# RWKV attention and fp4 feed-forward layer: the scores of all heads in one run, the down projection at the end of the step

## The reference

```
xx = [x(second row), x shifted by one row] - x
r, k, v = (x + xx*mix_{r,k,v}) @ W_{r,k,v}.T ;  g = sigmoid((x + xx*mix_g) @ W_g.T)
for each of 16 heads of width 16, over t:   state = state*w + k_t v_t^T ;  out_t = state r_t
y  = (out * g) @ W_o.T
x1 = layernorm(x + layernorm(y)*gamma + beta)
q(z) = blockwise fp4 quantise/dequantise, blocks of 16
h  = silu(q(x1) @ q(w_gate).T) * (q(x1) @ q(w_up).T)          (704 wide)
out = layernorm(x1 + q(h) @ q(w_down).T)
```

## Time and profile before

| | |
|---|---|
| median of 3 runs | 659.39 us (658.94 to 662.06) |
| profiled execution, its own time | 656.57 us |
| its span in the trace | 654.6 us |
| PE busy | 569.1 us (87%) |
| DVE busy | 510.9 us (78%) |
| POOL busy | 330.4 us (50%) |
| ACT busy | 277.2 us (42%) |
| mean granted clock | 0.959 of 2.4 GHz |

### The profile page before, as it was taken

One profiled execution on the slowest core, in us unless ns is written; L12 is line 12 of the kernel. 1 busy time (PEld: TensorE's weight loads), 2 busy tenths in 40 slices (PEclk: granted clock), 3 DMA queues, 4 the chain that ended last, 5 costly groups with the idle time before them and its releaser, 6 DMA issues.

```text
span 654.6 us, 14594 instructions
## 1 busy us (share of the span) xinstructions
PE 569.1 (87%) x5120; PEld 477.9 (73%) x5120; DVE 510.9 (78%) x1506; ACT 277.2 (42%) x637; POOL 330.4 (50%) x471
## 2 busy tenths in 40 slices
PE   1468589999999999999999999999999999987754
PEld 1356467888878888888888888888888888876643
DVE  2988667888878888888888888888788888778751
ACT  1235255444444455444445444444445544432211
POOL 2234344555555555555555555555565555544321
PEclk9687689999999999999999999999999999999896
DMA  7300000000000000000000000000000000000000
GB/s 191 102 2 1 9 10 3 1 18 17 19 17 18 18 17 19 18 17 18 17 11 9 17 18 19 18 17 17 18 18 18 9 11 10 9 10 10 9 9 20
DMA packets 14046, 13.13 MB, mean 20 GB/s; under 512 B 2576, under 2 KB 13712, under 8 KB 13968
## 3 DMA queue, kind: packets, MB, share of 16 engines
q1 hardware_dynamic: 13968, 12.13, 6.2%
HBM read 7.93 MB, written 4.19 MB: 19 GB/s over the span
## 4 chain that ended last, share of the span: by engine, by line
PE 79%; DVE 9%; ACT 5%; POOL 2%; issue 2%; DMA 1%; SPq 0%; DVEq 0%; POOLq 0%; ACTq 0%
PE bank L734 20%; PE bank L867 14%; PE bank L677 9%; PE bank L752 9%; PE bank L716 4%; PE bank L804 4%; PE bank L759 4%; PE bank L769 4%; PE bank L859 3%; ACT hq_t L591 3%; PE bank L704 2%; DVE mix L1044 2%; PE bank L694 1%; POOL rstd L353 1%; PE bank L814 1%
## 5 line engine op out<-in xcount | busy, mean ns | idle before, releaser
L371 POOL TENSOR_SCALAR_AFFINE_SELECT scores<-scores 128x512 f32<-128x512 f32 x128 | 89.0, 708 | 81.0 <-ACT scores L508 80.4
L867 PE MATMUL bank<-down_t,hq_t 128*128 128x256 f32 x384 | 94.1, 396 | 21.6 <-ACT hq_t L591 21.6
L353 POOL TENSOR_TENSOR rstd<-veps,neg_half 128x1 f32<-128x1 f32 x96 | 77.8, 810 | 66.9 <-DVE veps L994 66.1
L867 PEld LDWEIGHTS bank<-down_t,hq_t 128*128 128x128 f32 x384 | 72.0, 194 | 38.3 <-ACT hq_t L591 29.4
L1044 DVE SCALAR_TENSOR_TENSOR mix<-shift,mu,x_t 128x128 f32<-128x128 f32 x256 | 82.5, 374 | 2.6 <-POOL shift L380 2.6
L508 ACT COPY scores<-bank 128x512 f32<-128x512 f32 x128 | 68.8, 590 | 34.5 <-PE bank L677 32.7
L752 PE MATMUL bank<-mix,proj_t 128*128 128x128 f32 x512 | 70.2, 295 | 10.5 <-DVE mix L1044 10.5
L734 PE MATMUL bank<-gu_hi,xq_hi 128*128 128x352 f32 x256 | 68.4, 349 | 11.2 <-DVE late L1092 6.4
L380 POOL TENSOR_TENSOR shift<-x_t 128x256 f32<-128x256 f32 x32 | 20.1, 629 | 112.6 <-ACT x_t L529 111.3
L752 PEld LDWEIGHTS bank<-mix,proj_t 128*128 128x128 f32 x512 | 66.1, 209 | 12.1 <-DVE mix L1044 11.1
L677 PE MATMUL bank<-r_par,rv 32*128 32x256 f32 x512 | 72.5, 400 | 0.8 <-ACT scores L508 0.8
(11 more groups left out here) (123 smaller groups left out, 1160.2 us busy)
## 6 DMA issues: line engine op xcount, KB each, us to landing
x_tok<-in_L_attn_x_dram SPq DMA_DIRECT2D x32, 128.0 KB, 2.3
out_dram<-late_down SPq DMA_DIRECT2D x32, 128.0 KB, 1.7
late_down<-in_L_ffn_w_down_dram SPq DMA_DIRECT2D x1, 704.0 KB, 8.6
late<-in_L_ffn_w_gate_dram SPq DMA_DIRECT2D x1, 640.0 KB, 7.1
late<-in_L_ffn_w_up_dram SPq DMA_DIRECT2D x1, 640.0 KB, 7.3
scores<-in_L_attn_W_r_dram SPq DMA_DIRECT2D x1, 256.0 KB, 5.0
scores<-in_L_attn_W_v_dram SPq DMA_DIRECT2D x1, 256.0 KB, 5.3
scores<-in_L_attn_W_g_dram SPq DMA_DIRECT2D x1, 256.0 KB, 5.5
```

The lines of the kernel that those rows point to most:

```text
L353: g.tensor_tensor(rstd[:, i:i + 1], veps[:, i:i + 1], neg_half, ALU.pow).then_inc((rstd_ready, x_rstd, y_rstd)[i], 1)
L371: g.affine_select(out=a, in_=a, compare_op=ALU.is_ge, fill=0.0, base=0, pattern=[[0, 4], [1, P]], channel_multiplier=-1).then_inc(s_masked, 1)
L867: mm = t_.matmul(B_PA[:, 0:C], hq_t[:, t.c % 2, j], down_t[:, j], start=(j == 0), stop=(j == NH - 1))
```

## The change

- TensorE: the attention output (`outs_of`) now comes directly behind the state sums, and then the scores of all four quads in one run, into `B_PA`, `B_PB`, `B_S0` and `B_S1` (`s_bank`). Since `B_PA` and `B_PB` still hold r, v, g and k of `tile(1)`, the run waits for their readers: `rv_ready`, `r_par_ready`, `sg_ready`, `kd_ready`.
- TensorE: behind the first gate/up half come the transposes of hq (`tile(6)`), then that of v (`tile(1)`), then the second gate/up half, and the down projection last.
- ScalarE: the output norm ahead of the score copies; three score copies ahead of the first silu, the fourth behind it; then x1, the moves of hq_t, of v, and the second silu.
- GpSimd: the four masks together behind hq, the power of index 1 and gate_pow.
- VectorE: `norm1(1)`, `hgrid(3)`, `norm1(2)` and `u1` ahead of `norm3(2)`; `mix_of(R)` behind `norm2(1)`; `norm2(2)` ahead of `kd`; `mix_of(V)` behind `kd`.

```diff
--- before.py
+++ after.py
@@ -112,6 +112,7 @@
         bank = [ctx.enter_context(nc.psum_tensor(f"bank{i}", [P, 512], F32))[:] for i in range(8)]
         B_T, B_PA, B_PB, B_S0, B_S1, B_O, B_GATE, B_UP = bank
         w_bank = (B_GATE, B_UP)
+        s_bank = (B_PA, B_PB, B_S0, B_S1)
 
 
         ident = sb("ident", [P, P])
...
@@ -415,6 +410,8 @@
                                     ).then_inc(gate_pow_ready, 1)
                 t = None if general else tile(2)
                 if t is not None:
+                    mask(t, 0)
+                    mask(t, 1)
                     mask(t, 2)
                     mask(t, 3)
                 t = tile(4)
...
@@ -552,19 +549,23 @@
                     wait(act, tanh_ready, t.count(1, 1))
                     s.activation(sig_g[:, t.c % 2], sig_g[:, t.c % 2], ACT.Copy, bias=0.5, scale=0.5
                                  ).then_inc(sg_ready, 1)
+                t = tile(7)
+                if t is not None:
+                    wait(act, rstd2_ready, t.count(1, 1))
+
+                    wait(act, y_stored[t.c % 2], t.affine(16 * TPB // 2, 16 * (t.c // 2) + 1))
+                    normalised(y_out[:, t.c % 2], u2, 2, y_ready)
                 t = None if general else tile(2)
                 if t is not None:
                     score(t, 0)
                     score(t, 1)
-                t = tile(7)
-                if t is not None:
-                    wait(act, rstd2_ready, t.count(1, 1))
-
-                    wait(act, y_stored[t.c % 2], t.affine(16 * TPB // 2, 16 * (t.c // 2) + 1))
-                    normalised(y_out[:, t.c % 2], u2, 2, y_ready)
+                    score(t, 2)
                 t = tile(5)
                 if t is not None:
                     gate(t, 0)
+                t = None if general else tile(2)
+                if t is not None:
+                    score(t, 3)
                 t = tile(4)
                 if t is not None:
                     wait(act, x_norm_ready, t.count(1, 1))
...
@@ -592,6 +581,14 @@
                            ).then_inc(h_t_ready, 1)
                     s.copy(hq_t[:, t.c % 2, 4:6], B_PB[:, 0:256].rearrange("p (h n) -> p h n", h=2)
                            ).then_inc(h_t_ready, 1)
+                t = tile(1)
+                if t is not None:
+                    wait(act, v_tr, t.count(1, 1))
+                    wait(act, u_used, t.count(1, -3))
+                    s.copy(v_tok[:, t.c % 4], B_T[:, 0:C]).then_inc(v_tok_ready, 1)
+                t = tile(5)
+                if t is not None:
+                    gate(t, 1)
 
             act.wait_ge(flag_ready, 2)
             either_path(act, flag, lambda general: run_tiles(
@@ -664,17 +661,19 @@
             pe.wait_ge(w_moved, 5)
             pe.wait_ge(tabs_moved, 5)
 
-            def scores_of(t, half):
-
-                if half == 0:
-                    wait(pe, rv_ready, t.count(1, 1))
-                    wait(pe, r_par_ready, t.count(2, 2))
-                wait(pe, s_moved, t.count(QUADS, 2 * half))
+            def scores_of(t):
+
+                wait(pe, rv_ready, t.count(1, 2))
+                wait(pe, r_par_ready, t.count(2, 4))
+                wait(pe, sg_ready, t.count(1, 2))
+                wait(pe, kd_ready, t.count(1, 2))
+                wait(pe, ln2_step, t.count(LN2, 1 - 5 * LN2))
+                wait(pe, h_t_ready, t.count(2, -8))
+                wait(pe, s_moved, t.count(QUADS, 0))
                 for hf in range(KC):
-                    for i in range(2):
-                        q = 2 * half + i
+                    for q in range(QUADS):
                         rows = slice(32 * q, 32 * q + 32)
-                        mm = t_.matmul((B_S0, B_S1)[i][:, hf * 256:hf * 256 + 256],
+                        mm = t_.matmul(s_bank[q][:, hf * 256:hf * 256 + 256],
                                        rv[rows, t.c % 4, 1, hf],
                                        r_par[rows, t.c % 2, hf].rearrange("p r n -> p (r n)"),
                                        start=True, stop=True, skip_group_check=True)
@@ -743,6 +742,7 @@
                 wait(pe, rv_ready, t.count(1, 0))
                 if not general:
                     wait(pe, r_par_ready, t.count(2, 0))
+                    wait(pe, s_moved, t.count(QUADS, 2 - 2 * QUADS))
                 wait(pe, sg_ready, t.count(1, 0))
                 wait(pe, kd_ready, t.count(1, 0))
                 for i in (R, V):
@@ -821,36 +821,20 @@
                 t = None if general else tile(3)
                 if t is not None:
                     sums_of(t)
+                    outs_of(t)
                 t = None if general else tile(2)
                 if t is not None:
-                    scores_of(t, 0)
-                t = None if general else tile(3)
-                if t is not None:
-                    outs_of(t)
+                    scores_of(t)
                 t = tile(5)
                 if t is not None:
                     gate_up(t, 0)
-                t = tile(1)
-                if t is not None:
-                    wait(pe, rv_ready, t.count(1, 1))
-                    wait(pe, x_moved, t.count(1, 2))
-                    wait(pe, xq_t_ready, t.count(1, -3))
-                    wait(pe, v_tok_ready, t.count(1, 0))
-                    for k in range(KC):
-                        mm = t_.transpose(B_T[:, k * P:(k + 1) * P], rv[:, t.c % 4, 1, k], ident)
-                    mm.then_inc(v_tr, 1)
-                t = None if general else tile(2)
-                if t is not None:
-                    scores_of(t, 1)
-                t = tile(5)
-                if t is not None:
-                    gate_up(t, 1)
                 t = tile(6)
                 if t is not None:
                     wait(pe, hq_ready, t.count(1, 1))
                     wait(pe, rv_ready, t.count(1, 6))
                     if not general:
                         wait(pe, r_par_ready, t.count(2, 12))
+                        wait(pe, s_moved, t.count(QUADS, 4 * QUADS + 2))
                     wait(pe, sg_ready, t.count(1, 6))
                     wait(pe, kd_ready, t.count(1, 6))
                     wait(pe, ln2_step, t.count(LN2, 1 - LN2))
@@ -859,6 +843,18 @@
                         mm = t_.transpose(b[:, (j % 4) * P:(j % 4 + 1) * P],
                                           hq[:, t.c % 2, j * P:(j + 1) * P], ident)
                     mm.then_inc(h_tr, 1)
+                t = tile(1)
+                if t is not None:
+                    wait(pe, rv_ready, t.count(1, 1))
+                    wait(pe, x_moved, t.count(1, 2))
+                    wait(pe, xq_t_ready, t.count(1, -3))
+                    wait(pe, v_tok_ready, t.count(1, 0))
+                    for k in range(KC):
+                        mm = t_.transpose(B_T[:, k * P:(k + 1) * P], rv[:, t.c % 4, 1, k], ident)
+                    mm.then_inc(v_tr, 1)
+                t = tile(5)
+                if t is not None:
+                    gate_up(t, 1)
                 t = tile(6)
                 if t is not None:
                     for j in range(NH):
@@ -1143,15 +1139,13 @@
                                     B_T[:, 0:C].rearrange("p (k n) -> p k n", k=KC),
                                     xq_hi[:, t5.c % 2].bitcast(F32), ALU.subtract
                                     ).then_inc(xq_t_ready, 1)
-                mix_of(R)
-                norm3(2)
+                norm1(1)
                 hgrid(3)
-                norm1(1)
-                mix_of(V)
                 norm1(2)
                 if t4 is not None:
                     v.scalar_tensor_tensor(u1, B_GATE[:, 0:C], mv[:, 0, 0:1], gamma_b,
                                            ALU.subtract, ALU.mult).then_inc(ln_step, 1)
+                norm3(2)
                 hgrid(4)
                 if t4 is not None:
 
@@ -1165,6 +1159,8 @@
                 norm2(0)
                 hgrid(6)
                 norm2(1)
+                mix_of(R)
+                norm2(2)
                 if t1 is not None:
 
                     wait(dve, g_k_done, t1.count(1, 1))
@@ -1177,7 +1173,7 @@
                                         B_PB[:, C:2 * C].rearrange("p (a b i) -> p a b i", b=2, i=D),
                                         ipow.rearrange("p (a b i) -> p a b i", b=2, i=D), ALU.mult
                                         ).then_inc(kd_ready, 1)
-                norm2(2)
+                mix_of(V)
                 mix_of(G)
                 mix_of(K)
                 gated(0)
```

More of the change, by code:

```diff
@@ L409, in step @@
                                     per_block(h_scale, nb), ALU.mult).then_inc(hq_ready, 1)
+                t = tile(4)
+                if t is not None:
+                    rstd_of(t, 1, general)
                 t = tile(1)
@@ L554, in step @@
                                  ).then_inc(sg_ready, 1)
-                t = None if general else tile(2)
-                if t is not None:
-                    score(t, 0)
-                    score(t, 1)
```

(46 more changed lines are left out.)

8 lines of the change are left out of this document (1 added, 7 removed).

## The result

The changed kernel takes 764.33 us (762.28 to 765.03, 4 runs) against 659.70 for the one before (4 runs): ratio 1.157 (1.154 to 1.161), slower by 105 us. The direction was forecast, the size was not: 683 with a range from 668 to 714. The profiled execution took 765.03 us, span 763.3.

What follows compares the result with a forecast made beforehand. PE bounds the kernel at 17.53 us a step; -0.66 - 1.06 + 2.15 + 0.28 gives 18.24, taken as 18.4 given DVE's 19.08. 26 steps add 22.6 us, later ones 1.2: forecast 683 us, range 668 to 714.

Steps and rivals of the forecast that it cites:

- The wait for hq_t goes, 0.66: On PE ahead of the down projection: the wait for ScalarE's move of transposed hq disappears, minus 0.66 us a step.
- Four bands overlap, 1.06 us for all scores: On PE, scores of four quads in four row bands and banks overlap fully: 1.06 us for all, minus 1.06 a step.
- rival 3: PE's scores: four bands overlap no better than two, scores take 2.12 us, plus 27.6 us, 711 in all; chance 6%.
- Two powers in a row hold u: GpSimd's two consecutive powers take 1.77 us and delay VectorE's u to 409.33, against 409.08 before.
- The hold by L907: VectorE's L907 keeps the SBUF port and delays GpSimd's first power: 0.14 us a step more, 4 us over the run.
- `u` to `kd` takes 2.43 us today: On VectorE, R's mixes (0.53) and one veps (0.07) lengthen the stretch from u to kd to 3.03 us.
- PE goes on 0.04 us after `kd`: PE starts the scores 0.04 us after VectorE's kd ends, at 412.79, having waited 2.15 us since 410.64.
- The second wait, 0.28: PE waits for gated(0) ahead of the second gate/up half, plus 0.28 us a step.
- rival 2: PE's granted clock falls at the 2.15 us gap, 1.65 us a stretch: 697 us, or 726 in every step; chance 10%.
- The longer circle, 18.4: The longer of PE's circle (18.24 us) and DVE's through ScalarE (19.08, upper value) sets the step, taken as 18.4.
- Rival 1: The DVE circle in full with slow GpSimd powers sets the step: 19.4 us a step, 709 us in all; chance 17%.
- 26 steps, and nothing or 1.2 us outside them: New waits cost only in steps 7 to 32; steps 0 to 6 add nothing, steps 33 to 35 add 1.2 us.

Runs made afterwards that it cites:

- a_fill: Changed kernel plus eight unused 256-column matmuls on TensorE ahead of its wait for kd: 722.8 us, 1.097 of the kernel before.
- a_veps: Changed kernel with the output norm's veps (norm3(2)) back ahead of norm1(1) and hgrid(3): 733.8 us, 1.116 of the kernel before.
- a_pool: Changed kernel with GpSimd's hq behind the power of index 1, VectorE's order untouched: 718.4 us, 1.088 of the kernel before.
- a_pool_fill: Changed kernel with GpSimd's hq behind the power of index 1 and five unused matmuls ahead of TensorE's wait for kd: 692.1 us, 1.050 of the kernel before.
- a_kd: Changed kernel with kd directly behind norm2(1) on VectorE, norm2(2) and mix_of(R) behind it: 680.6 us, 1.031 of the kernel before.

## Why the prediction was wrong

Step by step, in the order in which it was argued.

- **The wait for hq_t goes, 0.66.** Right: the wait is gone, and alone it is worth 0.86 us a step (17.50 to 16.64), 0.2 more than forecast.
- **Four bands overlap, 1.06 us for all scores.** Right: 1.08 in a_fill at 2.4 GHz (rival 3 is out). The 1.13 that the prediction estimates beside it stands there without its working; 3.66 us, its own figure for sixteen full passes of 256 columns, would give 1.19 by the same factor.
- **Two powers in a row hold u.** Right to 0.04 us. That the place of one `veps` costs is confirmed by a_veps: 0.64 us of PE's gap, 0.97 us a step. The hold by L907, priced at 0.14 a step more, is not seen: the first power ends at 389.42, 0.41 after that instruction (389.01), and it needs 0.55 alone.
- **"`u` to `kd` takes 2.43 us today; R's mixes (0.53) and one `veps` (0.07) come in: 3.03."** This is the first step that failed: 4.14 in the trace (390.39 to 394.53). The prediction priced the mixes where they stood, with GpSimd idle or at a light operation, and moved them into the stretch in which `hq` now runs: `hq` waits for `hgrid(6)`, and only the short `norm2(1)` stands between that and the mixes. In the kernel before `hq` stood behind two masks and a power and began 2.2 us after the end of `hgrid(6)`, when the mixes were over:

```profile
413.70 1.38 POOL L408 TENSOR_TENSOR hq<-late,h_scale 128x704 f32<-128x704 f32 x1
```

The prediction did weigh how VectorE and GpSimd hold each other up, but only for the powers, and it costed GpSimd's reordering at nothing because GpSimd had idle time. a_pool gives the price: 1.13 us direct. Between a_fill and a_pool_fill the step differs by 1.30; less the 0.19 by which a_fill's matmuls outlast `kd` that is 1.1 again.
- **PE goes on 0.04 us after `kd`.** 0.31 to 0.34, in every kernel in which it waits there (394.94 to 395.25; 407.27 to 407.59 in a_kd). No row shown with the prediction gives 0.04 for VectorE and TensorE.
- **The second wait, 0.28.** 0.36 a step (6.9 / 19).
- **The clock, rival 2, 10%.** This is the second step that failed, and the larger error: the forecast has the fallen clock at nothing. The rival's mechanism and its rows were right (2.5 us without PE work was followed by 1.2 GHz); its chance hung on a gap of 2.15 us that became 3.4 (4.1 in one step of eight) with the two terms above. Its price, 1.65 us for a stretch, compares with 1.61 to 1.8 a step in a_fill. But even at 2.15 the chance was too low: the prediction put the border between gaps of 2.13 and 2.5 us, and the clock fell in about three steps of four with gaps of 2.27 (a_pool) and in one of three with 1.68 (a_kd). The errors were not independent, and the range had to treat them so: a term that lengthens the gap also raises the chance that the clock falls, and then both come in every step.
- **The longer circle, 18.4.** With the two away, 18.43 in a_pool_fill. That it hit so well is partly luck: 18.4 was chosen between 18.24 and 19.08. Rival 1 was right that a second circle comes close: ahead of `u2` VectorE waits for the down projection in 20 of 21 steps before, and in 3 of 19 after (1.1 us in all).
- **26 steps, and nothing or 1.2 us outside them.** 26 steps at 3.84 are 100 of the 108 us. "Steps 0 to 6: nothing" was wrong: PE waits for `kd` there too, 8.3 us in three waits, and step 7 begins 4.9 us later. The end is 11.6 us longer, two of the 26 steps included (7.7). So some 9 us lie outside, against 1.2 forecast; for the end the cause is open.

Against 18.4 forecast, the 2.94 us a step are thus 1.6 for the clock (changed kernel to a_fill) and 1.3 for the mixes beside `hq` (a_fill to a_pool_fill), or, with the 0.19 us of a_fill's own matmuls put back, about 1.8 and 1.1.

## What to carry to other kernels

Before a VectorE instruction is moved, look at what GpSimd does at the new place, and what GpSimd waits for: an operation that is released just ahead of the new place will start beside the moved instruction, as `hq` does here in each step that was looked at. When a forecast puts a new idle gap on TensorE, price the gap and the clock together, and raise the clock's chance with everything that could lengthen the gap. A change of several parts can hide a gain: one part alone was worth 14 to 15 us.
